# v projected with wv stationary in two column groups and turned back by transposes, values beside transposes, one ring count for the whole program

## What is computed

```
n = LN(x); q = n @ Wq; k = n @ Wk; v = n @ Wv        # 16 query heads, 4 key/value heads, 16 wide
q, k = rope(q), rope(k)
o = softmax(q k^T / sqrt(256)) v                      # every key head serves 4 query heads
x = x + LN(o @ Wo)
x = x + LN(LN(x) @ (ternary(weight) * alpha)^T + bias)
```

## Time and profile before

| what | value |
|---|---|
| median of 3 runs | 1492.5 us (1488.67 to 1494.1) |
| the profiled execution, its own time | 1492.92 us |
| its span in the profile | 1491.1 us |
| PE busy | 1431.0 us, 96% |
| DVE busy | 1337.7 us, 90% |
| ACT busy | 1240.0 us, 83% |
| POOL busy | 754.6 us, 51% |
| mean granted clock of PE | 0.978 of full speed |

### The profile page before, as it was taken

The page is one execution under the profiler, slowest core; times in us unless marked ns, Lnnn a source line. Parts: engine busy times, 40 slices in busy tenths (PEclk is TensorE's granted clock), DMA queues, the critical chain, the costliest instruction groups (busy, mean ns, idle before and its releaser), DMA issues.

```text
span 1491.1 us, 32225 instructions
## 1 busy us (share of the span) xinstructions
PE 1431.0 (96%) x12350; PEld 460.7 (31%) x12350; DVE 1337.7 (90%) x1471; ACT 1240.0 (83%) x2483; POOL 754.6 (51%) x1205
## 2 busy tenths in 40 slices
PE   6699999999999999999999999999999999999996
PEld 5122322223232332323222233323322232222236
DVE  5798999999999999999999999999999989999814
ACT  2079889898988989898898989898898989899881
POOL 4322275645665466745656555745656455363340
PEclk9589999999999999999999999999999999999999
DMA  3311121311212130221313122221311112121001
GB/s 106 102 48 48 33 71 41 98 34 50 70 60 66 51 80 23 87 53 46 79 36 94 31 72 48 78 63 41 76 41 55 39 60 66 36 66 31 30 23 44
DMA packets 72921, 84.92 MB, mean 57 GB/s; under 512 B 17632, under 2 KB 58464, under 8 KB 71328
## 3 DMA queue, kind: packets, MB, share of 16 engines
q1 hardware_dynamic: 71952, 82.08, 19.7%
q10 hardware_dynamic: 816, 0.79, 0.2%
HBM read 46.66 MB, written 24.64 MB: 48 GB/s over the span
## 4 chain that ended last, share of the span: by engine, by line
PE 73%; ACT 12%; DVE 7%; issue 4%; POOL 2%; DMA 1%; SPq 0%; POOLq 0%; ACTq 0%; DVEq 0%
PE pv L1017 28%; PE smax L995 27%; ACT probs L887 10%; DVE row_max L1267 5%; PE ring L1130 5%; PE ring L1041 3%; PE ring L1104 3%; PE ring L1118 2%; PE ring L1138 2%; ACT heads L951 1%; PE ring L1124 1%; PE ring L1065 1%; PE ring L1088 1%; ACT act L940 1%; PE smax L961 0%
## 5 line engine op out<-in xcount | busy, mean ns | idle before, releaser
L1267 DVE TENSOR_REDUCE row_max<-smax 128x1 f32<-128x1024 f32 x1024 | 1202.0, 1216 | 82.6 <-PE smax L995 73.1
L887 ACT ACTIVATE probs<-ring 128x512 f32<-128x512 f32 x2048 | 1103.9, 598 | 114.2 <-PE ring L1041 91.7
L995 PE MATMUL smax<-k_rows,q_rows 48*128 48x512 f16 x2048 | 631.3, 389 | 14.4 <-DVE row_max L1267 5.9
L1041 PE MATMUL ring<-q_rows,k_rows 50*128 50x512 f16 x2048 | 637.6, 384 | 3.5 <-DMA q_rows<-max_rows 1.6
L1017 PE MATMUL pv<-probs,v_cols 128*32 128x256 f32 (+1 forms) x6520 | 610.8, 447 | 11.7 <-ACT heads L951 11.3
L995 PEld LDWEIGHTS smax<-k_rows,q_rows 48*128 48x128 f16 x2048 | 115.7, 94 | 493.4 <-issue 293.6
L1017 PEld LDWEIGHTS pv<-probs,v_cols 128*32 128x32 f32 x6520 | 128.7, 108 | 331.6 <-issue 180.9
L1041 PEld LDWEIGHTS ring<-q_rows,k_rows 50*128 50x128 f16 x2048 | 132.7, 93 | 54.8 <-ACT probs L887 46.3
L577 POOL TENSOR_TENSOR attnT<-pairs,inv_rows 128x512 f32<-128x512 f32 x31 | 39.5, 1273 | 178.6 <-DMA inv_rows<-inv_sums_dram 178.6
L556 POOL TENSOR_TENSOR act<-act,bias_sb 128x256 f32<-128x256 f32 x60 | 42.3, 728 | 115.4 <-ACT act L940 115.4
L1130 PE MATMUL ring<-wo_sb,attnT 128*128 128x256 f32 x256 | 72.2, 407 | 3.9 <-DVE attnT L577 1.7
(11 more groups left out here) (166 smaller groups left out, 1130.0 us busy)
## 6 DMA issues: line engine op xcount, KB each, us to landing
q_stage_dram<-q_parts SPq DMA_DIRECT2D x45, 256.0 KB, 2.5
q_rows<-q_stage_dram SPq DMA_DIRECT2D x30, 384.0 KB, 5.9
x_in<-in_L_attn_x SPq DMA_DIRECT2D x8, 1024.0 KB, 6.1
pairs<-heads SPq DMA_DIRECT2D x64, 128.0 KB
inv_rows<-inv_sums_dram SPq DMA_DIRECT2D x32, 256.0 KB
res<-in_L_attn_x SPq DMA_DIRECT2D x16, 512.0 KB, 4.2
out<-res SPq DMA_DIRECT2D x15, 512.0 KB, 3.2
k_rows<-k_stage_dram SPq DMA_DIRECT2D x64, 96.0 KB, 3.2
```

Of the source, the lines that this page charges most:

```text
L887: eng.activation(probs[:, s % PSLOTS, j, :], ring[:, n % RING, :], ACT.Exp, scale=score_unit).then_inc(ring_read, 1)
L995: mm = eng.matmul(smax[:, side, c, :], q_rows[at:to, qc, kv * KVP + jp, qt * P:(qt + 1) * P], k_rows[at:to, kv, c * 512:(c + 1) * 512], st ...
L1041: eng.matmul(ring[:, n % RING, :], k_rows[at:to, g, kt * P:(kt + 1) * P], q_rows[at:to, h.qc, g * KVP + j // 2, :], start=True, stop=True)\
L1267: eng.tensor_reduce(row_max[:, g % 2, at:at + 1], smax[:, side, :, :].rearrange("p c n -> p (c n)"), AX.X, ALU.max).then_inc(max_read, 1)
```

## The change

- In the seven second halves that prepare a next batch, the four `V` jobs become two jobs. `VT` at step 5: wv stationary (64 columns), the transposed x moving in two blocks of 512 columns, the two results in two column groups of one bank (partitions 0 and 64 on). ACT copies it to a new buffer `vT`. `VN` at step 7: four transposes of `vT` back to token rows, which ACT writes to `v_next`. Steps 6 and 16 lose their `V` job; `Q` moves from step 15 to 16. The lone prologue keeps the old form.
- Where the job of a step is `XT`, `HT` or `VN`, the values are cut in two again, and the job stands ahead of the first values block. In a step s % 8 == 2 without a job the values stand whole behind i = 2.
- The ring's bank number runs on over the halves, and `ring_free` is the plain rule everywhere; `after` is gone.
- The statistics of x move from steps 5 to 8 to steps 5, 8, 9, 10, with three of them between the reductions of step 5.
- The store of the inverses stays at steps 4 and 22, its load back moves to steps 5 and 23, in SP's program behind the transfers of `MT` of that step.

```diff
-PRO1 = {5: [("V", 0)], 6: [("V", 1)], 7: [("V", 2)], 16: [("V", 3)],
-        15: [("Q", 1, 0)], 30: [("Q", 1, 1)]}
+PRO1 = {5: [("VT",)], 7: [("VN",)], 16: [("Q", 1, 0)], 30: [("Q", 1, 1)]}
...
-X_MOM_FIRST, X_MOM = (0, 1, 2, 3, 4, 5, 6, 7), (5, 5, 6, 6, 7, 7, 8, 8)
+X_MOM_FIRST, X_MOM = (0, 1, 2, 3, 4, 5, 6, 7), (5, 5, 5, 5, 8, 8, 9, 10)
...
-INVERT, SCALED = {22: 0, 4: -1}, {27: 0, 7: -1}
+INVERT, SPREAD, SCALED = {22: 0, 4: -1}, {23: 0, 5: -1}, {27: 0, 7: -1}
...
-ROOM = {"Q": 2, "K": 2, "V": 1, "WO": 1, "FF": 1}
+ROOM = {"Q": 2, "K": 2, "VT": 3, "WO": 1, "FF": 1}
...
     def values_at(self, s):
 
-        return {3: ALL} if self.jobs_behind(s, 1) else {1: (0, 1), 3: (1, 2)}
+        kinds = [job[0] for job in self.jobs_behind(s, 1)]
+        if kinds and kinds[0] not in ("XT", "HT", "VN"):
+            return {3: ALL}
+        if not kinds and s % KT == LAG:
+            return {2: ALL}
+        return {1: (0, 1), 3: (1, 2)}
...
     def ring_free(self, n):
 
-        if n >= RING:
-            return self.base + n - RING + 1
-        return self.base - min(((count - n - 1) % RING for count in self.after), default=0)
+        return self.base + n - RING + 1
...
+        vT = sb("vT", [P, HALF], F32)
...
-            def spread_inverses(h, pair):
+            def store_inverses(h, pair):
 
                 eng.wait_ge(inverted, h.pair0 + pair + 1)
-                at_least(eng, divided, h.pair0 + pair)
                 eng.dma_start(inv_dram[pair % DT, :, :].rearrange("j (k n) -> (j k) n", n=FOLD),
                               inv_sums[:, pair % DT, :]).then_inc(inv_stored, 16)
+
+            def spread_inverses(h, pair):
+
+                at_least(eng, divided, h.pair0 + pair)
                 eng.wait_ge(inv_stored, (h.pair0 + pair + 1) * 16)
...
                     if s in INVERT and (h.scores if INVERT[s] >= 0 else h.flush):
-                        spread_inverses(h, INVERT[s])
+                        store_inverses(h, INVERT[s])
...
                                .then_inc(max_loaded, 16)
+                    if s in SPREAD and (h.scores if SPREAD[s] >= 0 else h.flush):
+                        spread_inverses(h, SPREAD[s])
...
-                            eng.matmul(ring[:, n % RING, :],
+                            eng.matmul(ring[:, (h.base + n) % RING, :],
...
+                        if i == 1:
+                            n = projections(h, h.jobs_behind(s, i), n)
                         if i in parts:
                             values(h, s - LAG, *parts[i])
-                        n = projections(h, h.jobs_behind(s, i), n)
+                        if i != 1:
+                            n = projections(h, h.jobs_behind(s, i), n)
...
+                    elif kind == "VT":
+                        for dt in range(DT):
+                            for c in range(2):
+                                mm = eng.matmul(dst[c * SIDE:c * SIDE + HKV * HD, :], wv_sb[:, dt, :],
+                                                xT[:, dt, c * HALF:(c + 1) * HALF], start=(dt == 0), stop=(dt == DT - 1),
+                                                skip_group_check=True)
+                    elif kind == "VN":
+                        eng.wait_ge(ring_read, h.done("VT"))
+                        for t in range(ST):
+                            mm = eng.transpose(dst[:, t * P:(t + 1) * P], vT[:, t * P:(t + 1) * P], ident[:, :])
```

More of the change, by code:

```diff
@@ L143, in __init__ @@
     def __init__(self, b, qc, scores=True, maxima=STEPS, turned=range(1, HKV + 1), pro=None, pro1=None,
-                 epi=None, late=None, rot=None, base=0, first=0, steps=STEPS, load_x=None, mom=None, flush=True,
-                 after=()):
+                 epi=None, late=None, rot=None, base=0, first=0, steps=STEPS, load_x=None, mom=None, flush=True):
         self.b, self.qc = b, qc
@@ L165, in __init__ @@
         self.flush = flush
-        self.after = after
         self.alone = not scores and not maxima
@@ L380, in schedule @@
             at += h.count
-            n0 = h.count
-            n1 = Half(0, 1, pro1=0, epi=(0, 0)).count
-            n2 = Half(0, 0, pro=0, epi=(0, 0)).count
             for b in range(B - 2):
[L385 to L392, removed]
+                h = Half(b, 1, pro1=b + 1, epi=(b, 0), late=(b - 1, 1) if b > 0 else None, rot=(b + 1, 0),
+                         base=at, mom=b + 2)
+                half(h)
+                at += h.count
+                h = Half(b + 1, 0, pro=b + 2, epi=(b, 1), late=(b, 0), rot=(b + 1, 1),
+                         base=at, load_x=b + 3 if b + 3 < B else None)
+                half(h)
+                at += h.count
+            h = Half(B - 2, 1, pro1=LAST, epi=(B - 2, 0), late=(B - 3, 1), rot=(LAST, 0), base=at)
             half(h)
             at += h.count
-            h = Half(LAST, 0, epi=(B - 2, 1), late=(B - 2, 0), rot=(LAST, 1), base=at, after=(h.count,))
+            h = Half(LAST, 0, epi=(B - 2, 1), late=(B - 2, 0), rot=(LAST, 1), base=at)
             half(h)
             at += h.count
-            h = Half(LAST, 1, epi=(LAST, 0), late=(B - 2, 1), maxima=STEPS - LEAD, turned=range(1, HKV), base=at,
-                     after=(h.count,))
+            h = Half(LAST, 1, epi=(LAST, 0), late=(B - 2, 1), maxima=STEPS - LEAD, turned=range(1, HKV), base=at)
             half(h)
             at += h.count
-            h = Half(B, 0, scores=False, maxima=0, turned=(), epi=(LAST, 1), late=(LAST, 0), base=at,
-                     after=(h.count,))
+            h = Half(B, 0, scores=False, maxima=0, turned=(), epi=(LAST, 1), late=(LAST, 0), base=at)
             half(h)
@@ L823, in half @@
                     if h.scores and h.qc == 1 and s in V_TAKEN and h.b is not LAST:
-                        eng.wait_ge(ring_read, h.done("V", 3))
+                        eng.wait_ge(ring_read, h.done("VN"))
                         for g in V_TAKEN[s]:
@@ L886, in half @@
                             eng.wait_ge(ring_full, h.done("ST", s, j))
-                            eng.activation(probs[:, s % PSLOTS, j, :], ring[:, n % RING, :], ACT.Exp,
+                            eng.activation(probs[:, s % PSLOTS, j, :], ring[:, (h.base + n) % RING, :], ACT.Exp,
                                            scale=score_unit).then_inc(ring_read, 1)
@@ L903, in copy_jobs @@
                     kind, a = job[0], job[1:]
-                    src = ring[:, n % RING, :]
+                    src = ring[:, (h.base + n) % RING, :]
                     eng.wait_ge(ring_full, h.done(*job))
@@ L925, in copy_jobs @@
                         move(rot_in[:, 1, a[1], at:to], src[:, 0:to - at], 1.0 / (X_UNIT * W_UNIT))
+                    elif kind == "VT":
+                        move(vT[:, :], src, 1.0 / X_UNIT)
+                    elif kind == "VN":
+                        at_least(eng, v_ready, h.pro1 * HKV)
+                        move(v_next[:, :, :].rearrange("p (c t) n -> p t c n", c=2),
+                             src.rearrange("p (t c n) -> p t c n", t=ST, c=2))
                     elif kind == "V":
@@ L1052, in projections @@
                     kind, a = job[0], job[1:]
-                    dst = ring[:, n % RING, :]
+                    dst = ring[:, (h.base + n) % RING, :]
                     at_least(eng, ring_read, h.ring_free(n))
```

## The result

| what | before | after |
|---|---|---|
| median of 4 runs | 1491.1 us (1488.67 to 1494.1) | 1522.1 us (1520.9 to 1524.41) |
| span of the profiled execution | 1491.1 us | 1520.1 us |
| mean granted clock of PE | 0.978 | 0.967 |

The changed kernel takes 1.0209 of the time of before, 95% interval 1.0185 to 1.0233. That is 31 us more, where 14 were forecast. The sign was right, the size was not, and 1522 lies outside the range of 1496 to 1519.

The account below looks back on a forecast made before the run. The prediction took PE to bound steps with jobs, and PE and DVE together the plain ones. From 1492.9 us, +10.3 for the terms and +3.4 for the clock gave 1506.6, range 1496 to 1519.

Parts of the forecast that it names:

- the clock: PE's granted clock after waits at `WO`: falls at two of fourteen waits, +3.4 us; bounds 0 to +24.
- Rival (a): At the `WO` waits: the clock falls at most of them, eight or more, 1516 to 1527 us; chance 0.16.
- Ring: At the start of both halves: the waits for the restarted ring go, -0.80 us a pair (-0.55 and -0.25).
- v: `VT` adds 0.79 us at step 5, its two tiles side by side; steps 15 and 16 together give -0.89.
- rival (b): In `VT` at step 5: the two tiles run one after the other, 3.6 us, total 1518; chance 0.04.
- Transposes: In transpose steps: the values cover the bank wait of 0.29; `XT` -0.75 and `HT` -0.1 us a pair.
- Values behind i = 2: Steps 2, 18, 26 without a job: DVE gets its second maxima later, +0.55 us a pair.
- Step 6 to `WO`: From step 6 to `WO` of step 8: the later load back makes it 7.06 us in every half, +2.24 a pair.
- Sum: All terms without the clock: +1.04 us a pair, +6.2 for six pairs, +10.3 with the four other halves.
- (c): From issue to `WO`: the load back lands sooner, so no change, 1486 to 1499 us; chance 0.13.
- (d): From issue to `WO` only about 3.4 us, so the inverses don't hold PE up; 1480 to 1483, chance 0.05.

Follow-up runs that it names:

- e3: The changed kernel with eight extra matmuls (six in second halves), their product overwritten, ahead of PE's wait at `WO`; 1503.7 us, ratio 1.0092.
- e7: The changed kernel with load back at step 4, no values whole behind i = 2, and values whole behind i = 3 in all job steps; 1474.2 us.
- e8: The changed kernel with the load of x at step 12 instead of 6; 1516.9 us, ratio 1.0159.
- e2: The kernel before with only the load back of the inverses moved to step 5, behind `MT`'s transfers; 1515.3 us, ratio 1.0159.
- e1: The changed kernel with the load back of the inverses at step 4, ahead of `MT`'s transfers again; 1482.8 us, ratio 0.9957.

## Why the prediction was right in sign and wrong in size

The step that failed is "Whether one alone lowers the clock, no row says; bounds are none and all fourteen, 0 to +24. I take two, +3.4." Rival (a), given 0.16, came true: eleven falls, 18.7 us, or 17.1 more than before. e3 shows it apart from all other terms, 18.4 us. The price of one fall (1.7 from the earlier trace rows, measured 1.6) was right; the number of them wasn't. The rows that I had pointed the other way from my choice: a wait of 0.66 without a fall, 1.32 followed by 0.59 with one. A wait forecast at 1.4 to 1.8 was on the second one's side, and "they were two waits close together" was no reason to let it count for so little. Ten more falls than before at that price, and the same sum gives 1503.2 + 17 = 1520. The exact count couldn't have been forecast from the length of the waits: two waits of 1.44 went both ways.

Term by term (us; "pair" is a second and a first half, by the starts of the steps; where pairs differ a little, the commonest value stands):

- **Ring.** Forecast -0.80 a pair, measured -0.80 (-0.55 and -0.25).
- **v.** Step 5 +0.79 forecast, +0.83 measured; steps 15 and 16 -0.89, measured -0.89. The two 64 wide tiles run side by side: one row holds the eight matmuls, with the scores before and after it.

```profile
348.06 0.38 PE L1049 MATMUL ring<-q_rows,k_rows 50*128 50x512 f16 x1
348.37 1.94 PE L1126 MATMUL ring<-xT,wv_sb 128*64 128x512 f32 x8
350.24 0.39 PE L1049 MATMUL ring<-q_rows,k_rows 50*128 50x512 f16 x1
```

  From 348.37 to 350.24 is 1.87, not the 3.6 of rival (b).
- **Transposes.** `XT` -0.75 forecast, -0.84 measured; `HT` -0.1, measured about -0.2. A step takes 2.80 to 2.85. The forecast had a slip here: three steps at 2.80 against 2.95 are -0.45, not the -0.3 it put down for steps 3 to 5, and they measured -0.41. The Trainium skill's rule (TensorEngine Tiling (Array Packing), Key Properties) that a change of tiling mode drains the engine, which alone would have left no gain, didn't decide: e7 puts the new order at 7.2 us in all.
- **Values behind i = 2.** Forecast +0.55, measured +0.80: +0.34 and +0.44 in the second half, +0.24 in the first, and -0.11 twice. The mechanism stands in the timeline of the changed kernel's step 2: DVE waits for maxima that come behind the values, and then PE waits for DVE.

```profile
341.69 1.06 PE L1025 MATMUL pv<-probs,v_cols 128*32 128x512 f32 x8
...
342.92 0.38 PE L1003 MATMUL smax<-k_rows,q_rows 48*128 48x512 f16 x1
343.11 3.49 DVE L1288 TENSOR_REDUCE row_max<-smax 128x1 f32<-128x1024 f32 x3 [0.67 <-PE smax L1003]
...
344.39 0.39 PE L1003 MATMUL smax<-k_rows,q_rows 48*128 48x512 f16 x1 [0.31 <-DVE row_max L1288]
```

- **Step 6 to `WO`.** Forecast 7.06 in every half. Measured 7.10 on average in second halves. In the six first halves of full pairs 7.55 (8.14, 7.70, 7.77, 7.17, 7.31, 7.23): that the load of x would now start directly behind the load back stood in SP's order shown above, and I priced the landing by the earlier trace rows, where that load came behind two more transfers. e8 moves it away and gets 7.16. The Trainium skill (DMA: Bandwidth & Descriptors, Issuing engines are not separate DMA queues) says that transfers interleave on the same 16 engines. The 0.96 of DMA share in the wait and e8 fit that.
- **Sum.** Without the clock, the halves alone grew by 31.7 - 17.1 = 14.6 against +10.3 forecast. Of the 4.3 between them 2.6 lie in the stretch to `WO`, mostly the longer landing: fifteen of them grew by 16.9 in sum, where the forecast's terms give 14.3. The rest is mostly the values behind i = 2 (0.25 a pair). The start of the program was 2.5 shorter in this profiled run, which is chance.

Rivals (c) and (d) needed a faster way from issue to `WO`; it took 5.0 to 6.2 us.

## What to carry to other kernels

A store and its load back on a queue that other transfers share should be followed to the engine at the far end before anything is put in front of it: here one table entry cost 40 us in the changed kernel (27 in the one of before, e2), while all other edits together gained 8 (e1 against before, the halves alone). Count a wait of PE twice, once for its own length and once for what the clock takes afterwards, and if the trace shows only one wait of that size with a fall behind it, take a fall as the likely case. Where PE and DVE have the same beat, a block of work put between PE's two halves of DVE's input costs more than the short wait that it hides.

## What the runs showed of the hardware

The length of a wait doesn't settle whether the clock falls. Without a fall passed waits of 1.31, 1.43, 1.44 and 1.80 us (after), 2.01 (e8) and 2.06, 2.24 and 2.35 (e2); with one, 1.44, 1.50, 1.59, 1.64 and everything from 1.93 on (after). Waits up to 0.66 with no other wait of that size close by never had one; waits of 1.23 and 0.66 that ended 1.3 us apart had (e1). What else decides it was not tried; only that PE at work in the wait prevents it (e3), and that DMA traffic isn't needed for it (e8). The Trainium skill (TensorE: Matmul & The Clock Gate, HAM oscillation — how this bites in real kernels) warns of idle gaps of PE longer than these. Here one of 1.44 was enough, and the measurement decides.
